# Layer 0 of a two-layer FFT and box-filter kernel: the order of ten matmul rounds, and a seven-row sum on VectorE cut into quarters

## The chip, the cores and the metric

The kernel runs on one core of one Trainium2 chip. The metric is device time of one launch in microseconds, the median of several runs. One launch handles all eight images.

## The reference

The input x has shape (8, 16, 512, 512), float32. Both layers are residual blocks with a group norm (8 groups of 2 channels) in front:

```python
# layer 0: a 3x3 complex convolution in the frequency domain
X = jnp.fft.rfftn(gn(x), axes=(-2, -1)); Xr, Xi = jnp.real(X), jnp.imag(X)
Yr = rconv(Xr, wr) - rconv(Xi, wi) + b_real
Yi = rconv(Xr, wi) + rconv(Xi, wr) + b_imag
x = x + jnp.fft.irfftn(lax.complex(Yr, Yi), axes=(-2, -1))
# layer 1: a 15x15 mean filter, zero padded
x = x + mean_filter(gn(x), 15)
```

A 3x3 convolution of the spectrum is, back in the image, a product with a few sines and cosines of the place. The kernel uses this: it never forms a spectrum.

## The kernel before

**Layout.** The 128 partitions are 8 blocks of image rows times 16 channels, in two halves of 64. An image is 64 "rows" t = 0 to 63 of 128x512 in the tile `img`: row t holds one image row of each of the 8 blocks. After layer 0 a row t in `img` is the layer's output.

**Layer 0, one row n.** TensorE (PE) makes the row's Hilbert transform with 12 matmuls of 128x256 (L536, `front_hilbert`), one row ahead of where it needs it. Then comes `mix`: 40 matmuls of 64x512, in ten rounds of four. The array is used as four 64x64 tiles, so the four of a round run beside each other. Two of a round are "lower" (the operands in partitions 0 to 63, by the list `LOWER`), two are "upper" (partitions 64 to 127, by `UPPER`). They sum three results in PSUM: p0 ("base", with a last "wrap" term, L633), p1 ("cosine") and p2 ("sine"). Each result is opened by one half and closed by the other, three matmul pairs each: p1 is opened by lower cosine and closed by upper cosine, p2 is opened by upper sine and closed by lower sine, and the upper half of p0 is added during the next row's rounds (`late_base`). Between opening and closing PE waits for its own signal: `p1_half` (the last lower cosine pair is done) in front of round 6, `p2_half` (the last upper sine pair is done) in front of round 7. p1 and p2 have one buffer each, so their next opening waits until VectorE has read them: `t1_done` and `t2_done`. Rounds are counted from 0.

VectorE (DVE) takes a row in a "slot": two instructions for the first wave term from p1 (L1264, signal `t1_done`), two for the second from p2 (L1270, `t2_done`), then for the row before it the output row from p0 (L1279, waits for `q_done`) with its statistics (L1282), then the low part of the next row's Hilbert transform (L1222). GpSimd (POOL) makes a row in three additions: the low part of a later normalised row (L1412, f16), wave term 1 plus the image row (L1419), plus wave term 2 (L1422, `q_done`). ScalarE (ACT) normalises, copies the Hilbert transform's high part, and adds a constant to the finished row (`x1_whole`). The order within each engine is the order of the code; semaphores tie the engines.

**Loops.** Every engine runs slots 0 to 7 of a layer unrolled, then a hardware loop of 8 slots each turn, then the last 8 unrolled. On VectorE slots 8 to 15 were unrolled too (`slot(1, s, 1)`), because the head sum stands there. In a loop an instruction that addresses `img` or `bias_c` by row needs register work by the engine's sequencer.

**Head sum.** Layer 1 starts from `head`, the sum of rows 0 to 7. Slots 9 to 15 each end with one addition of 128x512 by `sum_head` (L1298 the first, L1301 the other six). The last one signals `presummed`, for which ScalarE waits after the layer's statistics.

## Time and profile before

| what | value |
|---|---|
| median of 3 runs | 3490.39 us (3487.72 to 3494.23) |
| the profiled execution | 3492.99 us |
| its span, first to last instruction | 3491.0 us |
| PE busy | 3107.4 us (89%) |
| VectorE busy | 3076.4 us (88%) |
| GpSimd busy | 2723.9 us (78%) |
| ScalarE busy | 2446.0 us (70%) |
| granted TensorE clock, mean | 0.980 |

The profile is of one execution. Busy time is the time in which an engine has an instruction in flight; instructions of VectorE overlap by some 0.08 us, so that a start can lie before the end of the one in front. A row of layer 0 takes about 3.8 us, and there are 512 of them. Layer 1 and the work between the layers fill the rest.

### The profile page before, as it was taken

What the parts mean: (1) busy time and instruction counts of PE and PEld (TensorE: products, weight loads), DVE (VectorE), ACT (ScalarE), POOL (GpSimd) and SP (SyncE); (2) the same over time, 40 slices, a digit from 0 to 9 for tenths busy, and PEclk for the clock granted to TensorE, in tenths of its full rate; (3) what the DMA queues carried; (4) which work ended last, traced back from release to release, by engine and by line L of the source; (5) the groups of instructions that cost most, each with busy time, mean ns of one, the idle gap of its engine ahead of it and who ended that gap; (6) DMA issues with size and microseconds to landing.
All of it is one profiled execution on the core that took longest, in us unless ns stands there. A gap on an engine that the chain in (4) does not pass through costs nothing.

```text
span 3491.0 us, 110788 instructions
## 1 busy us (share of the span) xinstructions
PE 3107.4 (89%) x36064; PEld 1869.7 (54%) x36064; DVE 3076.4 (88%) x5786; ACT 2446.0 (70%) x4742; POOL 2723.9 (78%) x2231
## 2 busy tenths in 40 slices
PE   2199979999889988899899998999988999899986
PEld 1155555555555555555555555555555555555555
DVE  6789978999889988899798997999978998889987
ACT  2568865787658876588666885578865787658876
POOL 4079975899749987599776997589974998759986
PEclk9699999999999999999999999999999999999999
DMA  8656668666876659766596666966678665876655
GB/s 206 200 93 128 127 202 252 114 127 120 249 205 126 128 116 285 169 125 128 154 293 125 126 129 184 272 113 128 120 225 229 117 128 119 259 195 126 127 129 174
DMA packets 726765, 573.58 MB, mean 164 GB/s; under 512 B 592416, under 2 KB 667776, under 8 KB 712064
## 3 DMA queue, kind: packets, MB, share of 16 engines
q1 hardware_dynamic: 704000, 451.67, 56.1%
q10 hardware_dynamic: 22400, 117.46, 13.1%
q8 instruction: 178, 2.92, 0.4%
q14 instruction: 187, 1.53, 0.2%
HBM read 262.08 MB, written 148.90 MB: 118 GB/s over the span
## 4 chain that ended last, share of the span: by engine, by line
PE 59%; DVE 16%; issue 9%; POOL 5%; DMA 3%; SPq 3%; ACT 1%; ACTq 1%; DVEq 0%; POOLq 0%
PE p L626 26%; PE h_ps L536 10%; PE h_odd L536 10%; DVE ob_all L1340 6%; DVE arena L1332 4%; PE p L633 4%; POOL arena L1479 3%; PE h_ps L626 3%; DMA out<-ob_all 2%; PE p L768 2%; DVE stat L1102 2%; PE h_ps L633 1%; PE p L575 1%; SPq L371 1%; ACTq L972 1%
## 5 line engine op out<-in xcount | busy, mean ns | idle before, releaser
L626 PE MATMUL p<-arena,bd_all 64*64 64x512 f16 x16896 | 1290.7, 381 | 31.2 <-DVE ob_all L1270 22.2
L626 PEld LDWEIGHTS p<-arena,bd_all 64*64 64x64 f16 x16896 | 555.2, 105 | 374.0 <-issue 233.1
L1419 POOL TENSOR_TENSOR ob_all<-ob_all,img 128x512 f32<-128x512 f32 x512 | 664.5, 1298 | 78.5 <-DVE ob_all L1264 52.2
L1422 POOL TENSOR_TENSOR ob_all<-ob_all 128x512 f32<-128x512 f32 x512 | 654.1, 1277 | 40.1
L1479 POOL TENSOR_TENSOR arena<-img 128x512 f32<-128x512 f32 x392 | 499.0, 1275 | 177.0 <-PE h_ps L757 97.9
L1264 DVE SCALAR_TENSOR_TENSOR ob_all<-p,bias_c,cosw 128x256 f32<-128x256 f32 x1024 | 447.6, 478 | 60.1 <-PE p L626 22.6
L886 ACT ACTIVATE img<-img,half_row (+1 forms) x1024 | 487.7, 528 | 5.0 <-ACT half_row L876 0.4
L768 PE MATMUL p<-band,arena 128*128 128x135 f16 (+1 forms) x4096 | 340.3, 228 | 154.9 <-DVE ob_all L1340 149.8
L1270 DVE SCALAR_TENSOR_TENSOR ob_all<-p,bias_c,cosw 128x256 f32<-128x256 f32 x1024 | 443.2, 474 | 0.0
L1412 POOL TENSOR_TENSOR arena<-arena 128x512 f16<-128x512 f32 x256 | 308.5, 1205 | 160.5 <-ACT arena L860 160.5
L859 ACT ACTIVATE arena<-img,sc 128x512 f16 (+1 forms) x512 | 433.8, 847 | 0.0
L944 ACT ACTIVATE arena<-arena,sc 128x512 f32<-128x512 f32 x392 | 282.9, 722 | 206.6 <-POOL arena L1479 197.9
L1340 DVE SCALAR_TENSOR_TENSOR ob_all<-p,img 128x512 f32<-128x512 f32 x512 | 347.5, 679 | 88.6 <-PE p L768 55.7
L1282 DVE BATCH_NORM_STATS2 stat<-img (+1 forms) x512 | 355.7, 695 | 51.7
L768 PEld LDWEIGHTS p<-band,arena 128*128 128x128 f16 x4096 | 260.5, 99 | 259.1 <-issue 244.6
L575 PE MATMUL p<-img,bd_all 128*64 128x256 f32 x2048 | 300.1, 402 | 92.6 <-POOL bd_all L1383 66.9
L536 PE MATMUL h_ps<-hilbert,arena 128*128 128x256 f16 x3072 | 379.8, 273 | 1.2 <-DMA arena<-arena 1.2
L536 PE MATMUL h_odd<-hilbert,xT_more 128*128 128x256 f16 x3072 | 379.8, 273 | 1.0 <-DMA xT_more<-arena 0.7
L1412 POOL TENSOR_TENSOR arena<-g_more,arena 128x512 f16<-128x512 f32 x256 | 311.7, 1218 | 55.5 <-ACT g_more L860 35.5
L536 PEld LDWEIGHTS h_odd<-hilbert,xT_more 128*128 128x128 f16 x3072 | 279.8, 98 | 138.2 <-issue 91.5
L536 PEld LDWEIGHTS h_ps<-hilbert,arena 128*128 128x128 f16 x3072 | 280.2, 98 | 132.6 <-issue 98.7
L1102 DVE BATCH_NORM_STATS2 stat<-img 128x6 f32<-128x512 f32 x512 | 334.8, 680 | 0.3
(182 smaller groups left out, 5136.6 us busy)
## 6 DMA issues: line engine op xcount, KB each, us to landing
out<-ob_all SPq DMA_DIRECT2D x512, 256.0 KB, 4.5
bd_all<-bd_dram SPq DMA_DIRECT2D x512, 224.0 KB, 2.5
img<-in_x ACTq DMA_DIRECT2D x168, 512.0 KB, 6.9
img<-in_x ACTq DMA_DIRECT2D x112, 256.0 KB, 5.3
img<-in_x SPq DMA_DIRECT2D x24, 512.0 KB, 26.1
arena<-img SPq DMA_DIRECT2D x48, 256.0 KB, 3.2
arena<-img SPq DMA_DIRECT2D x48, 192.0 KB, 2.7
bd_dram<-ob_all SPq DMA_DIRECT2D x11, 768.0 KB, 3.6
```

The source lines that it names most:

```text
L536: m = mm(dst(a), row[:, 4 * lx + k, :], tb["hilbert16"][:, lt, k, 0:cols], start=(half == 0 and i == 0), stop=(half == 1 and i == 2))
L626: m = mm(bank[out_half * HP:(out_half + 1) * HP, :], bd[s % RB][rows, 6 * lm + (j if own else j + 1), :], part, start=opens and i3 == 0, s ...
L768: m = mm(p0[0][:, lo:hi], parts[u % 3][:, l, k, :], tb["band16"][:, lo - k * P + R:hi - k * P + R], start=(u == 0 and k == 0 and l == 0), ...
L859: nc.scalar.activation(halves(gp[s][:, 0, :]), row, ACT.Identity, bias=sc[:, 9:10], scale=sc[:, 8:9])
L886: ins = nc.scalar.activation(row, row, ACT.Identity, bias=half_row[:, s, a:a + 1])
L1264: ins = V.scalar_tensor_tensor(t1[:, a, :], p1[:, a * HALF:(a + 1) * HALF], bias_c[:, 1, t, 1 - a:2 - a], cosw[:, a, :], ALU.subtract, ALU ...
L1270: ins = V.scalar_tensor_tensor(t2[:, a, :], p2[:, a * HALF:(a + 1) * HALF], bias_c[:, 0, t, 1 - a:2 - a], sinw[:, a, :], ALU.add, ALU.mult)
L1340: V.scalar_tensor_tensor(ob[j % NS][:, u % 2, :], p0[0], 1.0 / (K * K * BOX_SCALE), img[:, u, :], ALU.mult, ALU.add).then_inc(row_out, 1)
L1412: G.tensor_tensor(gp[s][:, 1, :], g32[s % 2], gp[s][:, 0, :], ALU.subtract).then_inc(g_split, 1)
L1419: G.tensor_tensor(q, term_row[s % 2][0], parity(img[:, t, :]), ALU.add).then_inc(first_added, 1)
L1422: G.tensor_tensor(q, q, term_row[s % 2][1], ALU.add).then_inc(q_done, 1)
L1479: G.tensor_tensor(diff_row(u), more, less, ALU.subtract).then_inc(moved, 1)
```

## The change

`LOWER` is put in another order: base step 0, then the three cosine steps, then base steps 1 and 2. `UPPER` stays. The wait for `t1_done` moves to round 1, where lower cosine now opens p1; the wait for `t2_done` stays in round 2, where upper sine opens p2. Each has its own signal to `mix_step` (an instruction on PE's sequencer that nobody waits for).

The head sum starts from a memset and becomes 32 additions of 128x128: each slot from 8 to 39 adds one quarter of one row. So four slots handle one row, and the four turns of a new loop handle rows 0 to 7. Slots 8 to 15 are no longer unrolled on VectorE. `presummed` is now signalled by VectorE's sequencer after a wait for all 36 steps.

```diff
-LOWER = [("base", 0), ("base", 1), ("cosine", 0), ("cosine", 1), ("cosine", 2),
+LOWER = [("base", 0), ("cosine", 0), ("cosine", 1), ("cosine", 2), ("base", 1),
          ("base", 2), ("wrap", 3), ("sine", 0), ("sine", 1), ("sine", 2)]
...
-                        if r == min(LOWER.index(("cosine", 0)), UPPER.index(("sine", 0))):
+                        if r == LOWER.index(("cosine", 0)):
                             pe.wait_ge(t1_done, PRIMED + n)
+                            pe.sem_inc(mix_step, 1)
+                        if r == UPPER.index(("sine", 0)):
                             pe.wait_ge(t2_done, PRIMED + n)
                             pe.sem_inc(mix_step, 1)
...
-                def sum_head(t):
-
+                HEAD_OPS = NQ * (R + 2)
+
+                def clear_head():
+
+                    for q in range(NQ):
+                        V.memset(head[:, q * P:(q + 1) * P], 0.0).then_inc(head_chain, 1)
+
+                def sum_head(i, s):
+
+                    t = (i - 1) * (NG // NQ) + s // NQ
+                    cols = slice(s % NQ * P, (s % NQ + 1) * P)
                     dve.wait_ge(x1_whole, b * T + t + 1)
-                    if t == 1:
-                        ins = V.tensor_tensor(head, img[:, 0, :], img[:, 1, :], ALU.add)
-                    else:
-                        dve.wait_ge(head_chain, b * (R - 1) + t - 1)
-                        ins = V.tensor_tensor(head, head, img[:, t, :], ALU.add)
-                    ins.then_inc(head_chain if t < R else presummed, 1)
+                    dve.wait_ge(head_chain, b * HEAD_OPS + (i - 1) * NG + s + 1)
+                    V.tensor_tensor(head[:, cols], head[:, cols], img[:, t, cols], ALU.add).then_inc(head_chain, 1)
...
-                for s in range(NG):
-                    slot(1, s, 1)
-                    if s > 0:
-                        sum_head(s)
-                with dve.Fori(2, T // NG - 1) as i:
+                clear_head()
+                summed = 1 + (R + 1) * NQ // NG
+                with dve.Fori(1, summed) as i:
                     for s in range(NG):
-                        slot(i, s, 2)
+                        slot(i, s, 1)
+                        sum_head(i, s)
+                dve.wait_ge(head_chain, (b + 1) * HEAD_OPS)
+                dve.sem_inc(presummed, 1)
+                with dve.Fori(summed, T // NG - 1) as i:
+                    for s in range(NG):
+                        slot(i, s, summed)
```

What moves on PE, in the rounds of row 1: first the order before. The names are p1 and p2 (in the wave terms), p0_0 for the base of the row before, and h_ps for the base of this row (its buffer lies there); L633 are the wrap terms, round 6.

```order
L626 MATMUL h_ps<-arena,bd_all 64x512 x2
L626 MATMUL p0_0<-arena,bd_all 64x512 x2
L626 MATMUL p1<-arena,bd_all 64x512 [waits t1_done,t2_done]
L626 MATMUL p1<-arena,bd_all 64x512
L626 MATMUL p2<-arena,bd_all 64x512 x2
L626 MATMUL p1<-arena,bd_all 64x512 x2
L626 MATMUL p2<-arena,bd_all 64x512 x2
L626 MATMUL p1<-arena,bd_all 64x512 x2
L626 MATMUL p2<-arena,bd_all 64x512 x2
L626 MATMUL h_ps<-arena,bd_all 64x512 x2
L626 MATMUL p0_0<-arena,bd_all 64x512 x2
L633 MATMUL h_ps<-wrap_row,bd_all 64x512 [waits p1_half]
```

These are the rounds 1 to 6, four matmuls each. The same place now, from the first matmul of round 1:

```order
L626 MATMUL p1<-arena,bd_all 64x512 [waits t1_done]
L626 MATMUL p1<-arena,bd_all 64x512
L626 MATMUL p0_0<-arena,bd_all 64x512 x2
L626 MATMUL p1<-arena,bd_all 64x512 [waits t2_done]
L626 MATMUL p1<-arena,bd_all 64x512
L626 MATMUL p2<-arena,bd_all 64x512 x2
L626 MATMUL p1<-arena,bd_all 64x512 x2
L626 MATMUL p2<-arena,bd_all 64x512 x2
L626 MATMUL h_ps<-arena,bd_all 64x512 x2
L626 MATMUL p2<-arena,bd_all 64x512 x2
L626 MATMUL h_ps<-arena,bd_all 64x512 x2
L626 MATMUL p0_0<-arena,bd_all 64x512 x2
```

The three pairs on p1 stand one round earlier, one pair on h_ps has moved from round 1 to round 4, and p2 stays where it was. L633 with its wait for p1_half follows as before.

On VectorE, the end of a slot with a head sum and the start of the next, before:

```order
L1282 BN_STATS stat<-img 128x6 [waits x1_done]
L1221 REGISTER_ALU
L1222 SCALAR_TENSOR_TENSOR arena<-h_ps,arena 128x512 [waits h_kept]
L1300 REGISTER_ALU [waits x1_whole]
L1301 TENSOR_TENSOR arena<-arena,img 128x512 [waits head_chain]
L1264 SCALAR_TENSOR_TENSOR ob_all<-p1,bias_c,cosw 128x256 [waits p1_ready,q_done]
```

And now, in the loop over slots 8 to 39 (lines are shifted by two to eight):

```order
L1284 BN_STATS stat<-img 128x6 [waits x1_done]
L1223 REGISTER_ALU
L1224 SCALAR_TENSOR_TENSOR arena<-h_ps,arena 128x512 [waits h_kept]
L1308 REGISTER_ALU [waits x1_whole]
L1309 ISA [waits head_chain]
L1309 TENSOR_TENSOR arena<-arena,img 128x128
L1266 ISA [waits p1_ready,q_done]
L1266 SCALAR_TENSOR_TENSOR ob_all<-p1,bias_c,cosw 128x256
```

The addition has a quarter of the columns and stands in 32 slots instead of 7; the rows marked ISA are register work for addresses.

## Rows read from the trace of the kernel before

**Rows 1.** The page: busy us (share of the span) and instructions by engine
```profile
PE 3107.4 (89%) x36064; PEld 1869.7 (54%) x36064; DVE 3076.4 (88%) x5786; ACT 2446.0 (70%) x4742; POOL 2723.9 (78%) x2231
```
**Rows 2.** Image 3 by stretches: length, busy PE, PEld, DVE, ACT, POOL; clock, DMA
```profile
1456.87:1479.80 22.93, 21.52 (x300) 12.16 (x292) 21.63 (x42) 16.63 (x35) 21.27 (x18) 1.00 0.67 115
1479.80:1605.57 125.77, 124.72 (x1669) 71.34 (x1666) 119.39 (x231) 106.15 (x225) 121.14 (x97) 1.00 0.67 126
1605.57:1666.90 61.33, 61.33 (x832) 35.29 (x831) 57.55 (x112) 52.79 (x113) 58.94 (x48) 1.00 0.66 128
1666.90:1697.43 30.53, 29.35 (x410) 17.04 (x408) 28.23 (x57) 21.01 (x52) 27.35 (x24) 1.00 0.56 102
```
**Rows 3.** Timeline of PE (start us, length us): a row in the loop, one unrolled
```profile
1595.35 0.40 PE L626 MATMUL h_ps<-arena,bd_all 64*64 64x512 f16 x2
...
1595.59 0.38 PE L626 MATMUL h_ps<-arena,bd_all 64*64 64x512 f16 x2
...
1596.45 0.40 PE L626 MATMUL h_ps<-arena,bd_all 64*64 64x512 f16 x2
...
1596.79 0.40 PE L633 MATMUL h_ps<-wrap_row,bd_all 64*64 64x512 f16 x2
...
1465.84 1.49 PE L626 MATMUL p<-arena,bd_all 64*64 64x512 f16 x24
1467.26 0.40 PE L633 MATMUL p<-wrap_row,bd_all 64*64 64x512 f16 x2
```
**Rows 4.** Timeline of PE's weight loads in the same looped row
```profile
1595.77 0.39 PEld L626 LDWEIGHTS p<-arena,bd_all 64*64 64x64 f16 x12 [0.28 <-issue]
...
1596.76 0.14 PEld L633 LDWEIGHTS h_ps<-wrap_row,bd_all 64*64 64x64 f16 x2 [0.38 <-issue]
```
**Rows 5.** Timeline of DVE in looped rows
```profile
1594.05 0.88 DVE L1264 SCALAR_TENSOR_TENSOR ob_all<-p,bias_c,cosw 128x256 f32<-128x256 f32 x2
1594.84 0.86 DVE L1270 SCALAR_TENSOR_TENSOR ob_all<-p,bias_c,cosw 128x256 f32<-128x256 f32 x2
1595.62 0.74 DVE L1279 SCALAR_TENSOR_TENSOR img<-p,sc,ob_all 128x512 f32 x1
1596.50 0.69 DVE L1282 BATCH_NORM_STATS2 stat<-img  x1
...
1597.89 0.88 DVE L1264 SCALAR_TENSOR_TENSOR ob_all<-p,bias_c,cosw 128x256 f32<-128x256 f32 x2
```
**Rows 6.** Timeline of DVE in slots with a head sum
```profile
1490.79 0.67 DVE L1222 SCALAR_TENSOR_TENSOR arena<-h_odd,arena 128x512 f16<-128x512 f32 x1
1491.38 0.72 DVE L1301 TENSOR_TENSOR arena<-arena,img 128x512 f32<-128x512 f32 x1
1492.02 0.86 DVE L1264 SCALAR_TENSOR_TENSOR ob_all<-p,bias_c,cosw 128x256 f32<-128x256 f32 x2
...
1495.57 0.78 DVE L1301 TENSOR_TENSOR arena<-arena,img 128x512 f32<-128x512 f32 x1
1496.26 0.47 DVE L1264 SCALAR_TENSOR_TENSOR ob_all<-p,bias_c,cosw 128x256 f32<-128x256 f32 x1
```
**Rows 7.** Timeline of POOL: before and in the head slots, and a looped row
```profile
1483.50 1.16 POOL L1412 TENSOR_TENSOR arena<-arena 128x512 f16<-128x512 f32 x1
...
1491.52 1.60 POOL L1412 TENSOR_TENSOR arena<-arena 128x512 f16<-128x512 f32 x1
...
1596.54 1.27 POOL L1422 TENSOR_TENSOR ob_all<-ob_all 128x512 f32<-128x512 f32 x1
```
**Rows 8.** DVE with POOL idle: small additions (ns: shortest/median/longest), a full one, a memset
```profile
181.29 0.49 DVE L1173 TENSOR_TENSOR kappa<-kappa,trig_h 128x128 f32<-128x128 f32 x2
...
L1173 DVE TENSOR_TENSOR kappa<-kappa,trig_h x16: 282/288/292, 181.3 to 3105.5; 128x128 f32<-128x128 f32 x16
...
191.59 0.69 DVE L1217 TENSOR_TENSOR ob_all<-ob_all 128x512 f32<-128x512 f32 x1
...
2.42 0.30 DVE L1013 MEMSET img<- 128x288 f32 x1
```

## The prediction

> **What bounds the kernel now.** I read the page first: TensorE (PE), VectorE (DVE) and GpSimd (POOL) are all busy 78 to 89% of the span, so the mean names no bound [rows 1]. The change touches only the first layer, 64 rows of each of 8 images, so I cut the layer of one image into stretches at the starts of L1264 (the first wave term of a row) [rows 2]. From one of these starts to the next is one row's period; the starts are those of rows 1, 7, 39, 55 and 63 of image 3. Per row that gives 22.93/6 = 3.82 us, 125.77/32 = 3.93, 61.33/16 = 3.83 and 30.53/8 = 3.82. In the third stretch PE is busy for all of its 61.33 us, DVE for 57.55 and POOL for 58.94: there PE sets the pace, and the others follow 4 to 6% behind. The other images repeat this picture.
>
> PE spends 3.84 us on such a row (the start of L1264 moves from 1594.05 to 1597.89 [rows 5]). Of its ten rounds, counted from 0, round 0 starts at 1595.35 and round 1 at 1595.59 [rows 3]. From round 1 to round 5 (1596.45) it takes 0.86/4 = 0.215 us a round, but from round 5 to round 6 (1596.79) 0.34. Round 6 is where the wrap terms and the second half of the cosine sums start, behind the wait for p1_half; the weight loads show the same hole as 0.38 us of idle in front of L633 [rows 4]. p1_half is signalled by the last lower cosine matmul, in round 4, only two rounds before, and a matmul takes 0.38 to 0.40 us from start to end [rows 3]; what is left over is signal and load. So PE waits 0.34 - 0.215 = 0.12 us of each row for its own pipeline. In an unrolled row (1 to 7 and 55 to 63 are like it) round 6, L633 at 1467.26, comes 1.42 us after round 0, L626 at 1465.84, where an even pace (0.24 for the first step, then five at 0.215) makes 1.32: 0.10 us there [rows 3].
>
> A second loop is as long: t2 ends at 1594.84 + 0.86 = 1595.70, PE loads the weights of round 2 at 1595.77, DVE opens the next row's t1 at 1597.89 and ends its t2 1.65 later at 1599.54, 3.84 us after the last one [rows 4, 5]. The piece of it on PE, rounds 2 to 8, contains the same hole. In the rows 9 to 15, where a whole row is added to the head, DVE is the bound instead: L1264 to L1264 is 4.24 us with no idle time (1492.02 to 1496.26) [rows 6].
>
> **Part 1: the lower order.** It removes nothing and adds one wait with its signal per row on PE's sequencer. Lower cosine moves from rounds 2 to 4 to rounds 1 to 3, so p1_half is signalled a round (0.215 us) earlier and the 0.12 us hole in front of round 6 closes. p2_half stays in round 4 but is wanted only in round 7. Before, its signal came with p1_half, in time for a load at 1596.76 [rows 4], in front of round 6. An even pace would put round 7 at 1596.45 + 0.43 = 1596.88: 0.1 us to spare, so it should not open a hole of its own. The separated waits: t1 has ended at 1594.05 + 0.88 = 1594.93, 0.66 us before round 1, and t2 is still asked for at round 2, as before, so the new wait at round 1 costs nothing; queued behind it on PE are only that round's loads and matmuls. PE's own row falls to 3.72 us, and the loop through t2 as well (3.84 - 0.12).
>
> What is late next? DVE: 57.55/16 = 3.60 busy, 0.14 us in front of L1282 (1595.62 + 0.74 to 1596.50), less the 0.08 us by which L1301 starts before L1222 ends when nothing holds it: 3.66 [rows 2, 5, 6]. POOL: 58.94/16 = 3.68 busy, plus at most the 0.08 us between its two adds, and 0.05 of overlap to win back: 3.71 to 3.76 [rows 2, 7]. POOL may be a little over 3.72, but it may also lag: its sum of a row ends at 1597.81 and DVE wants it for its next L1279, at 1595.62 + 3.84 = 1599.46, 1.65 us later [rows 5, 7]. A few hundredths over some 24 rows fit in, and in the last stretch POOL is idle for 30.53 - 27.35 = 3.2 us in which it can catch up [rows 2]. So I take 3.72 for every row without a head sum. The gain: 6 x 0.10 = 0.6 us in the first stretch; in the third from 61.33 to 16 x 3.72 + 0.1 (a loop's turn) = 59.6, which is 1.7; 7 x 0.10 = 0.7 in the last. Together **3.0 us an image**.
>
> **Part 2: the head sum in quarters.** It removes 7 DVE additions of 128x512 and adds 32 of 128x128 and 4 memsets. Each quarter ends a slot, behind L1222, so DVE then needs 3.66 + q a row; that is above 3.72 for any q over 0.06: all 32 rows become DVE's, and PE's gain is lost in them. The price q: the trace has a 128x128 addition, L1173, of 0.28 us; two take 0.49 together, so the second starts 0.21 after the first, with POOL idle [rows 8]. Beside POOL it costs more: the full addition L1217 takes 0.69 alone, 0.61 without the overlap of 0.08, whereas in the head rows L1301 holds DVE 0.64 (1491.38 to 1492.02) and 0.69 [rows 6, 8]. That adds 0.03 to 0.08, and I don't know whether it shrinks with the size. So q is 0.21 to 0.30; I take 0.26, the small row with the surcharge nearly whole. 32 x (3.66 + 0.26) = 125.4 us. To this come four turns of the loop, for which I take 0.1 each, an estimate from the 0.14 that register work costs in front of L1282 [rows 5], and the memsets: 0.30 for 288 columns, so about 0.15 each for 128 and 0.6 for four [rows 8]. They stand where DVE idles for PE anyhow, (22.93 - 21.63)/6 = 0.2 us a row [rows 2], so 0.4 remains. Sum 126.2 against 125.77: **0.5 us an image lost**, from 1.1 won (q = 0.21) to 1.7 lost (q = 0.30). The waits for x1_whole (a row finished several slots ago) and head_chain (DVE's own addition a slot ago) are met long before, and their register work fits beside L1282 and L1222 (1.3 us). The wait behind the loop, ahead of presummed, costs one drain.
>
> **Sum.** 3.0 - 0.5 = 2.5 us an image, 20 us for eight. The profiled execution took 3492.99 us with a span of 3491.0; it lies 2.6 above the median of 3490.39, and nothing outside the rows changes, so I subtract from the median: **3470**. With the ends of q: 8 x 4.1 = 33 and 8 x 1.3 = 10 us, 3457 to 3480.
>
> **Rivals.** (a) *The hole only moves.* If p2_half reaches the sequencer too late, round 7 waits the 0.10 to 0.12 us that round 6 waited. For it: the 0.1 us to spare is no more than the hole itself, worked out from ends that are modelled. Then Part 1 gives nothing: 3490 + 8 x 0.5 = 3494, and 3504 with q = 0.30. If half of the hole stays, 3482.
>
> (b) *GpSimd pays by the piece, and the kernel gets slower.* Under a full addition L1412 takes 1.60 to 1.61 us instead of 1.16, 0.45 more: it began at 1491.52, and DVE's addition ran from 1491.38 to 1492.10, so it stood still about while DVE added [rows 6, 7]. A quarter should cost it about 0.11. If the price were per instruction, POOL would need 3.75 + 0.45 = 4.20 a row for 32 rows, 134.4 less the lag of 1.65 = 132.8 against 125.8: 7 us an image, 56 - 24 = 32 slower, 3522. It decides from about 0.22 us a quarter (3.75 + 0.22 - 1.65/32 = 3.92). Against it: the 0.45 is within the time that the addition itself runs. The Trainium skill, GPSIMD Engine Reference, section 8, Key points, says that GpSimd shares its SBUF interfaces with VectorE instructions that have two SBUF inputs, as these additions do; by that rule the stall follows the instruction's running time, and the 1.61 beside 1.16 agrees.
>
> (c) *No overlap around the small additions.* If a quarter lets neither neighbour overlap it, q is 0.28 + 0.08 = 0.36: 32 x 4.02 + 0.8 = 129.4, 3.7 lost, 0.7 net, 3496. Against it: the two L1173 overlap by 0.07 us [rows 8]. The Trainium skill, VectorE: DVE Perf Modes, section The DRAIN you can't avoid, says that the next operation does not start until the pipe is empty; it speaks against cutting one addition into four, and would give this case. The overlapping starts of L1173 speak against it here.
>
> **How the numbers follow.** The forecast (hole closed, q 0.21 to 0.30) has 0.66; half of the hole stays, or POOL holds the rows near 3.78, 3481 to 3488, 0.10; rival (a) 0.09; (b) 0.07; (c) 0.05; better than 3457, if some wait goes that I did not see, 0.03. About 0.2% (7 us, 3483.4) is what a measurement of this kernel can tell from no change. Faster by more than that: 0.66 + 0.03 and half of the 0.10, 0.74. Within it: the rest of the 0.10, (c), and (a) with a small q, 0.16. Slower: (b) and part of (a), 0.10. The range for 8 in 10 takes the forecast, the half-closed hole and a little below: 3455 to 3488.
>
> **What would show it.** In the rows 39 to 63 the period should be 3.72 instead of 3.83, with no hole in front of L633's loads (0.38 idle before them would fall to the 0.1 or so of other rounds); a hole that moves to the round after it is (a). In the rows 7 to 39 L1264 to L1264 should be an even 3.90 to 3.95 with DVE hardly idle; 3.96 or more is (c), and a DVE that waits for L1422 with L1412 near 1.6 us in every row is (b). The quarter's duration should be 0.28 to 0.37 us. I am wrong in the whole if DVE's rows come out below 3.85 or PE's above 3.80.

## The result, and the profile after

The changed kernel takes **3463.16 us** (median of 4 runs, 3460.56 to 3468.07), the kernel before 3491.05 beside it (4 runs, 3487.72 to 3494.23). The ratio is 0.9919, with a 95% interval of 0.9907 to 0.9931: 28 us faster, 0.8%. 3470 was predicted, from 3455 to 3488.

The page of the changed kernel (span 3466.0 us, granted clock 0.978) gives nearly the same busy shares in its first row, which answers to [rows 1]:

```profile
PE 3085.5 (89%) x36064; PEld 1877.5 (54%) x36064; DVE 3077.9 (89%) x6018; ACT 2447.4 (71%) x4742; POOL 2713.3 (78%) x2231
```

Cut as in [rows 2], at the starts of the first wave term (now L1266) of rows 1, 7, 39, 55 and 63, an image without a disturbance (image 4) reads:

```profile
1862.61:1885.15 22.54, 21.13 (x302) 12.38 (x299) 22.09 (x46) 16.85 (x36) 21.11 (x18) 1.00 0.64 118
1885.15:2009.19 124.04, 123.74 (x1673) 72.00 (x1672) 118.87 (x257) 106.89 (x225) 120.94 (x97) 1.00 0.68 128
2009.19:2069.28 60.09, 59.62 (x827) 34.88 (x824) 57.48 (x113) 52.06 (x112) 58.03 (x48) 1.00 0.65 129
2069.28:2098.78 29.50, 28.60 (x410) 16.86 (x408) 28.20 (x56) 20.98 (x51) 27.07 (x23) 1.00 0.53 105
```

Against the forecast, as medians over the eight images:

| rows | before | predicted | after |
|---|---|---|---|
| 1 to 7 | 22.92 | 22.3 | 22.55 |
| 7 to 39 (head sum) | 125.76 | 126.2 | 124.20 |
| 39 to 55 | 61.32 | 59.6 | 60.08 |
| 55 to 63 | 30.52 | 29.8 | 29.50 |
| sum | 240.52 | 237.9 | 236.33 |

The forecast had 0.4 for the memsets in the second stretch; they lie at the end of the first. So without them the first stretch would be 22.1.

**The hole in front of the wrap terms is gone.** PE's timeline, rounds 2 to 8 of an unrolled row of after, answers to the last two rows of [rows 3]:

```profile
1449.56 1.05 PE L626 MATMUL p<-arena,bd_all 64*64 64x512 f16 x14 [0.37 <-DVE ob_all L1272]
1450.24 0.38 PE L626 MATMUL h_ps<-arena,bd_all 64*64 64x512 f16 x2
1450.42 0.41 PE L633 MATMUL p<-wrap_row,bd_all 64*64 64x512 f16 x2
```

Round 2 starts at 1449.56 and round 6, L633, at 1450.42: four rounds in 0.86 us, 0.215 each, with nothing left over. In a looped row the weight loads of L633 had 0.38 us of idle before them [rows 4]; now it is 0.16:

```profile
1626.84 0.60 PEld L626 LDWEIGHTS p<-arena,bd_all 64*64 64x64 f16 x16 [0.33 <-issue]
1627.61 0.14 PEld L633 LDWEIGHTS p<-wrap_row,bd_all 64*64 64x64 f16 x2 [0.16 <-issue]
```

**VectorE in the quarter rows** (its timeline in a slot of the new loop, answers to [rows 6]):

```profile
1517.19 0.87 DVE L1266 SCALAR_TENSOR_TENSOR ob_all<-p,bias_c,cosw 128x256 f32<-128x256 f32 x2
1517.97 0.87 DVE L1272 SCALAR_TENSOR_TENSOR ob_all<-p,bias_c,cosw 128x256 f32<-128x256 f32 x2
1518.76 0.74 DVE L1281 SCALAR_TENSOR_TENSOR img<-p,sc,ob_all 128x512 f32 x1
1519.64 0.69 DVE L1284 BATCH_NORM_STATS2 stat<-img  x1
1520.25 0.67 DVE L1224 SCALAR_TENSOR_TENSOR arena<-h_odd,arena 128x512 f16<-128x512 f32 x1
1520.84 0.28 DVE L1309 TENSOR_TENSOR arena<-arena,img 128x128 f32<-128x128 f32 x1
1521.04 0.87 DVE L1266 SCALAR_TENSOR_TENSOR ob_all<-p,bias_c,cosw 128x256 f32<-128x256 f32 x2
```

A row is 1521.04 - 1517.19 = 3.85 us. The quarter runs for 0.28 us, and the next instruction starts 0.20 after it: q = 0.20. The only idle time is the 0.14 in front of L1284. GpSimd's L1423, which begins while the quarter runs, takes 1.21 to 1.30 us in nearly all of the 256 such slots, 1.23 in the median, instead of 1.16 [rows 7].

**Two places cost more than I had thought.** The end of the new loop, in front of row 39's slot:

```profile
1594.07 0.28 DVE L1309 TENSOR_TENSOR arena<-arena,img 128x128 f32<-128x128 f32 x1
1594.96 0.88 DVE L1266 SCALAR_TENSOR_TENSOR ob_all<-p,bias_c,cosw 128x256 f32<-128x256 f32 x2 [0.61 <-DVE arena L1309]
```

and the memsets, in front of row 7:

```profile
1469.15 0.67 DVE L1224 SCALAR_TENSOR_TENSOR arena<-h_ps,arena 128x512 f16<-128x512 f32 x1
1469.80 0.59 DVE L1301 MEMSET arena<- 128x128 f32 x4
1470.31 0.75 DVE L1266 SCALAR_TENSOR_TENSOR ob_all<-p,bias_c,cosw 128x256 f32<-128x256 f32 x2
```

The row that ends in the first takes 4.55 us instead of 3.85, the row that ends in the second 4.12 instead of 3.70.

### The profile page after: what moved, and what is told of

Same layout as the page of the kernel before. It is cut to its first block, busy times and chain, and to the rows that moved or that the text cites. A ratio compares the mean times of both kernels' runs of the same rounds, so it can differ in the third digit from the quotient of the medians.

```text
span 3466.0 us, 112555 instructions
## 1 busy us (share of the span) xinstructions
PE 3085.5 (89%) x36064; PEld 1877.5 (54%) x36064; DVE 3077.9 (89%) x6018; ACT 2447.4 (71%) x4742; POOL 2713.3 (78%) x2231
## 4 chain that ended last, share of the span: by engine, by line
PE 43%; DVE 19%; issue 14%; POOL 10%; SPq 7%; DMA 5%; ACT 1%; ACTq 1%; DVEq 1%; POOLq 0%
PE p L626 19%; PE h_ps L536 7%; PE h_odd L536 7%; DVE ob_all L1351 5%; POOL arena L1490 4%; SPq L417 3%; DVE arena L1343 3%; PE p L770 3%; DMA out<-ob_all 3%; PE h_ps L626 2%; DVE stat L1104 2%; POOL ob_all L1433 2%; DVE ob_all L1272 2%; PE p L633 2%; POOL ob_all L1430 2%
## 5 line engine op out<-in xcount | busy, mean ns | idle before, releaser
L626 PE MATMUL p<-arena,bd_all 64*64 64x512 f16 x16896 | 1263.2, 380 | 25.3 <-DVE ob_all L1266 14.2
L1433 POOL TENSOR_TENSOR ob_all<-ob_all 128x512 f32<-128x512 f32 x512 | 653.4, 1276 | 40.1
L1266 DVE SCALAR_TENSOR_TENSOR ob_all<-p,bias_c,cosw 128x256 f32<-128x256 f32 x1024 | 445.9, 477 | 22.3 <-PE p L626 9.1
L1423 POOL TENSOR_TENSOR arena<-arena 128x512 f16<-128x512 f32 x256 | 309.2, 1208 | 162.0 <-ACT arena L862 162.0
L1284 DVE BATCH_NORM_STATS2 stat<-img (+1 forms) x512 | 355.6, 695 | 58.6
L1423 POOL TENSOR_TENSOR arena<-g_more,arena 128x512 f16<-128x512 f32 x256 | 307.5, 1201 | 58.3 <-ACT g_more L862 38.2
```

The costliest lines, as they stand in the source:

```text
L626: m = mm(bank[out_half * HP:(out_half + 1) * HP, :], bd[s % RB][rows, 6 * lm + (j if own else j + 1), :], part, start=opens and i3 == 0, s ...
L1266: ins = V.scalar_tensor_tensor(t1[:, a, :], p1[:, a * HALF:(a + 1) * HALF], bias_c[:, 1, t, 1 - a:2 - a], cosw[:, a, :], ALU.subtract, ALU ...
L1423: G.tensor_tensor(gp[s][:, 1, :], g32[s % 2], gp[s][:, 0, :], ALU.subtract).then_inc(g_split, 1)
L1433: G.tensor_tensor(q, q, term_row[s % 2][1], ALU.add).then_inc(q_done, 1)
```

## The experiments

Every kernel is compared with the kernel before on its own chip. The runs are from several chips: the kernel before had a median of 3490.13 us beside `order_only`, `quarters_only`, `split_old_order` and `late_signal`, 3492.28 beside `paired_wait`, `no_head`, `order_paired` and `all_three`, and 3492.32 beside the other four. Two kernels from different groups are therefore compared to some 2 us at best. A ratio as recorded can differ from the quotient of the two medians by up to 0.0012. The stretches given are medians over the eight images, in the order of the table above. Where a kernel starts from the changed kernel I say "after", where from the old one "before".

**Theory:** the lower order closes PE's hole, and that is the gain; the quarters cost DVE 0.20 us in 32 rows against 0.4 to 0.5 in 7, and give back a little; the row-38 stop and the split waits take some of it. **Rivals:** the gain comes from the separated waits, or from the spread head sum.

### Each half alone

`order_only`: before, with the new `LOWER` and the separate waits; the whole-row head sum stays.

```diff
-LOWER = [("base", 0), ("base", 1), ("cosine", 0), ("cosine", 1), ("cosine", 2),
+LOWER = [("base", 0), ("cosine", 0), ("cosine", 1), ("cosine", 2), ("base", 1),
...
+                        if r == LOWER.index(("cosine", 0)):
+                            pe.wait_ge(t1_done, PRIMED + n)
+                            pe.sem_inc(mix_step, 1)
```

> The kernel before with the new lower order and the separated waits alone; the head sum stays whole, in slots 9 to 15. Theory (the hole in front of round 6 was the gain, and the quarters take part of it back): the hole is gone in all rows but the seven that VectorE holds at 4.24 us. The unrolled rows fall from 3.83 to 3.70, the looped ones from 3.84 to 3.77 (as seen in the changed kernel, where round 2 starts 0.147 us after t2 ends instead of 0.101), among them the 24 rows 15 to 39, which the quarters hold at 3.86 in the changed kernel. Per image 0.5 + 1.8 + 1.25 + 1.0 = 4.6 us, 37 for eight: about 3454, which is less than the changed kernel's 3463. Rival (both parts are needed, since the gain of the order is only reached where the head sum is spread): no better than 3463.

Measured: 3456.57 us, ratio 0.9896 (0.9880 to 0.9912). It is 34 us faster than before, more than both parts together, where 37 had been expected. Its windows in image 5:

```profile
2271.94:2294.06 22.12, 20.73 (x296) 12.21 (x296) 21.61 (x42) 16.15 (x35) 20.70 (x17) 1.00 0.69 105
2294.06:2417.86 123.80, 121.42 (x1669) 72.38 (x1666) 119.26 (x232) 106.28 (x225) 120.89 (x98) 1.00 0.69 131
2417.86:2477.93 60.07, 60.07 (x833) 35.47 (x831) 57.48 (x112) 52.92 (x113) 58.70 (x49) 1.00 0.65 131
```

The looped rows without a head sum take 3.77 us, the seven with a whole addition 4.24, as before.

`quarters_only`: after, with the old `LOWER` and the joint wait.

```diff
-LOWER = [("base", 0), ("cosine", 0), ("cosine", 1), ("cosine", 2), ("base", 1),
+LOWER = [("base", 0), ("base", 1), ("cosine", 0), ("cosine", 1), ("cosine", 2),
...
-                        if r == LOWER.index(("cosine", 0)):
+                        if r == min(LOWER.index(("cosine", 0)), UPPER.index(("sine", 0))):
```

> The changed kernel with the lower order and the waits of before: the head sum in quarters alone. Theory: VectorE needs 3.66 + 0.20 = 3.86 us in the 32 rows, hardly over the 3.84 that PE needs with its hole, so the rows 7 to 39 take 32 x 3.86 = 123.5, plus 0.7 for the stop at the end of the new loop and 0.4 for the memsets, 124.4 to 124.6 against 125.77: 1.2 us an image, 10 for eight, about 3481. The other stretches stay at 61.3 and 30.5. Rival (a small addition costs 0.26 or more, as I had predicted): 126.2 for the stretch, 3494.

Measured: 3482.43 us, ratio 0.9972 (0.9958 to 0.9987). The second stretch is shorter than before, 124.7 for 125.8, and the first is 0.2 longer by the memsets (23.1 for 22.9); the other two are as before:

```profile
1477.47:1602.30 124.83, 124.25 (x1672) 71.73 (x1670) 118.96 (x258) 106.85 (x225) 120.90 (x97) 1.00 0.68 128
1602.30:1663.63 61.33, 60.79 (x827) 34.66 (x824) 57.58 (x113) 52.12 (x112) 58.25 (x48) 1.00 0.65 127
```

So the quarters win 8 to 10 us over the old order, and lose about 7 over the new one (3463 against 3457): with the hole closed, 3.77 is to be had in the 25 rows that need no head sum, and the quarters hold 32 rows at 3.85.

### The separated waits alone

`split_old_order`: before, the order kept; the wait for `t1_done` stands in round 1 with its own signal.

```diff
-                        if r == min(LOWER.index(("cosine", 0)), UPPER.index(("sine", 0))):
+                        if r == 1:
                             pe.wait_ge(t1_done, PRIMED + n)
+                            pe.sem_inc(mix_step, 1)
+                        if r == UPPER.index(("sine", 0)):
                             pe.wait_ge(t2_done, PRIMED + n)
```

> The kernel before with one edit: the wait for t1_done stands in round 1 with a signal of its own, t2_done stays in round 2, the order of the matmuls and the head sum stay. Theory (a wait for one semaphore costs PE's sequencer 0.05 us after the semaphore has come, a wait that follows another in one instruction does not): round 2 starts 0.147 us after t2's end instead of 0.101, so the 40 looped rows outside the head sum go from 3.84 to 3.89, 1.8 us an image, 15 for eight: 3505. Unrolled rows, where PE does not wait for t2, stay at 3.83. Rival (the 0.046 comes from the order of the matmuls): 3490, no change.

Measured: 3505.30 us, ratio 1.0037 (1.0023 to 1.0050), slower by 15 us. The looped rows go from 3.84 to 3.89, the unrolled ones stay at 3.82:

```profile
1614.83:1676.88 62.05, 62.05 (x832) 35.35 (x831) 57.59 (x112) 52.80 (x113) 58.91 (x48) 1.00 0.65 127
```

So the gain doesn't come from the waits; they cost. What they do is seen in the instruction on PE's weight-load sequencer that signals `mix_step` behind the wait for `t2_done`. The answers are for L696 of before, L698 of after and L699 of the kernel `paired_wait` below; the numbers are shortest/median/longest ns:

```profile
L696 PEldq EVENT_SEMAPHORE  x512: 51/789/791, 194.8 to 3365.5; - x171
```
```profile
L698 PEldq EVENT_SEMAPHORE  x512: 51/51/51, 196.1 to 3340.9; - x171
```
```profile
L699 PEldq EVENT_SEMAPHORE  x512: 51/639/642, 193.8 to 3335.3; - x171
```

I read these durations so: with two waits in front of it the instruction is begun at the first one and sits in flight until t2 is done; with a single wait it begins only when that semaphore has come, and its 51 ns then stand in front of round 2. `paired_wait` tests that: after, with a second wait for `t1_done`, met long before, ahead of the one for `t2_done`.

```diff
                         if r == UPPER.index(("sine", 0)):
+                            pe.wait_ge(t1_done, PRIMED + n)
                             pe.wait_ge(t2_done, PRIMED + n)
```

> The changed kernel with one line more: in round 2 PE waits for t1_done again, which has long come, and then for t2_done, so that the instruction that signals mix_step has two waits in front of it, as it had before the change. Theory (the 0.147 us from t2's end to round 2 are 0.05 of an instruction that only starts when its single semaphore comes; behind a second wait it is started already): 0.101 us again, the looped rows without a head sum fall from 3.77 to 3.72, 16 a image, 0.8 us, 6 for eight: 3457; the 32 rows with a quarter stay at 3.86, since VectorE holds them. Rival (the extra time belongs to two signals to mix_step in a row, or to the loads' new place): 3463.

Measured: 3460.91 us, ratio 0.9907 (0.9890 to 0.9923), and the looped rows that DVE doesn't hold are as expected, 3.72 us. Its third stretch, and t2 with the load of round 2 in one row (DVE and the weight loads):

```profile
1592.40:1651.91 59.51, 59.04 (x827) 34.91 (x825) 57.15 (x112) 52.03 (x112) 57.59 (x48) 1.00 0.65 130
```
```profile
1622.99 0.86 DVE L1273 SCALAR_TENSOR_TENSOR ob_all<-p,bias_c,cosw 128x256 f32<-128x256 f32 x2
```
```profile
1623.92 0.60 PEld L626 LDWEIGHTS p<-arena,bd_all 64*64 64x64 f16 x16 [0.28 <-issue]
```

t2 ends at 1623.85 and the load starts 0.07 later, as before (1595.70 to 1595.77 [rows 4, 5]). In after, t2 ends at 1625.86 + 0.87 = 1626.73 and the load follows at 1626.84, 0.11 later. Round 2's first matmul starts 0.147 us after t2's end in after and 0.102 here. An added wait that is always met makes each of these rows 0.05 us shorter. It does so only where PE waits for t2 and VectorE isn't the bound, in the 16 rows 39 to 54: their stretch falls from 60.08 to 59.50. That should be 5 us for eight images, and 3457 was expected. The 3460.91 don't show it: they are 2 us under after, inside the interval of the ratio, and the profiled execution lost two images' time to a fallen clock (below), after one. The rows are shown, the gain in time isn't.

### What the head sum costs

`no_head`: after, without the 32 additions, so that the head sum stays zero; that part of the computation is left out.

```diff
                         slot(i, s, 1)
-                        sum_head(i, s)
-                dve.wait_ge(head_chain, (b + 1) * HEAD_OPS)
+                dve.wait_ge(head_chain, (b + 1) * NQ)
```

> The changed kernel without the 32 additions; the memsets stay, so the head sum is zero and this part of the computation is left out. Theory (the quarters hold VectorE, and nothing else holds the rows 7 to 39): these rows fall from 3.86 to the 3.77 of the others, 32 x 0.085 = 2.7 us an image, 22 for eight: 3441. Rival (the new loop, its register work or GpSimd holds them): they stay near 3.86 and the time at 3463.

Measured: 3438.18 us, ratio 0.9848 (0.9826 to 0.9869). The looped rows take 3.77 but for the turn at row 14 (below). The price of the whole head sum in after is 25 us. By the second stretch it is 3.0 an image (124.20 less 121.16): 31 rows by 0.085, which is 2.6, and the stop, 4.55 for 3.77 in row 38, make 3.4; PE's waits for DMAs, a little longer here, hide some of it (row 14 is 4.14 here, 4.06 in after). Row 38 has lost its stop although the wait for the memsets still stands there: what costs is a wait for an instruction that is still running, and not the change of loops.

`late_signal`: after, with the wait for the last quarter and the signal `presummed` moved behind the second loop.

```diff
-                dve.wait_ge(head_chain, (b + 1) * HEAD_OPS)
-                dve.sem_inc(presummed, 1)
                 with dve.Fori(summed, T // NG - 1) as i:
                     for s in range(NG):
                         slot(i, s, summed)
+                dve.wait_ge(head_chain, (b + 1) * HEAD_OPS)
+                dve.sem_inc(presummed, 1)
```

> The changed kernel with the wait for head_chain and the signal presummed moved from the end of the summing loop to the end of the following loop. Theory (VectorE's row 38 takes 4.55 us instead of 3.86 because its sequencer must wait for the last quarter to end before it may start the next loop's register work): row 38 falls to about 3.86, 0.6 to 0.7 us an image, 5 for eight: 3458. Rival (the change of loops itself costs it): 3463, row 38 stays.

Measured: 3455.07 us, ratio 0.9888 (0.9869 to 0.9906), 8 us better than after where 5 were expected. The second stretch is 0.89 us shorter in each image (123.31 for 124.20), which is 7 for eight. Row 38 gives 0.70 of it. The rest is row 14, at the first turn of the new loop: its median is 4.06 us in after and 3.86 here. In after PE waits there for the DMAs of the transposed rows in five of eight images, by 0.2 to 1.1 us, here in one. I hadn't expected that, and why it comes in that row, and more often in after, is open. VectorE at the same place, without the stop:

```profile
1588.43 0.28 DVE L1309 TENSOR_TENSOR arena<-arena,img 128x128 f32<-128x128 f32 x1
1588.63 0.87 DVE L1266 SCALAR_TENSOR_TENSOR ob_all<-p,bias_c,cosw 128x256 f32<-128x256 f32 x2
```

Row 38 is 3.85 instead of 4.55. The wait for DVE's own last instruction had kept the next loop's register work from running under it; that the register work is what fills the 0.61 us is argued, that the wait causes them is shown.

`halves`: after with the late signal and the paired wait, and the head sum in 16 additions of 128x256 in slots 8 to 23.

```diff
...
-                    t = (i - 1) * (NG // NQ) + s // NQ
-                    cols = slice(s % NQ * P, (s % NQ + 1) * P)
+                    t = (i - 1) * (NG // NH2) + s // NH2
+                    cols = slice(s % NH2 * 2 * P, (s % NH2 + 1) * 2 * P)
...
```

> As the kernel with the late signal and the paired wait, but with 16 additions of 128x256 in slots 8 to 23, two memsets. Theory (a piece holds VectorE 0.07 us and 0.13 for each 128 columns: 0.20 for a quarter as measured, so 0.33 for a half, 0.60 to 0.65 for a whole): 16 rows at 3.66 + 0.33 = 3.99 and 16 at 3.72 are 123.4 for the rows 7 to 39, as 32 at 3.86 are 123.4: no difference to the quarters, 3449. Rival (a small piece has no price of its own, only its columns count): the halves would be worse than the quarters only by the slack they waste, and a half would measure 0.39 or more.

Measured: 3450.64 us, ratio 0.9888 (0.9868 to 0.9907). Here is VectorE around a half:

```profile
1071.47 0.42 DVE L1311 TENSOR_TENSOR arena<-arena,img 128x256 f32<-128x256 f32 x1
1071.80 0.87 DVE L1267 SCALAR_TENSOR_TENSOR ob_all<-p,bias_c,cosw 128x256 f32<-128x256 f32 x2
```

(In these lines, and in `paired_wait` above, t1 is L1267 because of the added line.) A half holds DVE 0.33 us, a quarter 0.20, a whole row 0.63 to 0.71 (two of them in [rows 6]). Summed over a row of the image that is 0.80 in quarters, 0.66 in halves and about 0.67 whole. Against a row of 3.72 that DVE could nearly keep (3.66), each slot with a piece loses q - 0.06: 32 x 0.14 = 4.5 us an image in quarters and 16 x 0.27 = 4.3 in halves. The slots with a whole addition are unrolled and don't have the idle time in front of the statistics, so they take 4.24 and lose 0.52 each, 7 x 0.52 = 3.6. The second stretches agree: 123.26 us in `late_paired` (quarters), 123.21 in `halves`, 122.84 in `order_paired_again` (whole). The pieces also need their memsets in the first stretch, 22.5 against 22.1. So the whole additions are the cheapest by 0.8 us an image, since DVE has only those 0.06 us a row to give.

### Why round 4 was early enough, and round 5 is not

`p2_late`: `order_only` with upper sine's last pair in round 5 instead of 4, two rounds ahead of round 7, where p2_half is wanted.

```diff
...
-UPPER = [("base", 0), ("base", 1), ("sine", 0), ("sine", 1), ("sine", 2),
-         ("base", 2), ("cosine", 0), ("cosine", 1), ("cosine", 2), ("wrap", 3)]
+UPPER = [("base", 0), ("base", 1), ("sine", 0), ("sine", 1), ("base", 2),
+         ("sine", 2), ("cosine", 0), ("cosine", 1), ("cosine", 2), ("wrap", 3)]
```

> The kernel with the new lower order and the whole head sum, but with the last upper sine pair moved from round 4 to round 5, so that p2_half is signalled two rounds ahead of round 7, as p1_half was of round 6 in the kernel before. Theory (a signal of PE to itself needs more than two rounds, less than three): a hole of 0.10 to 0.12 us in front of round 7 in every row, the unrolled rows back from 3.70 to 3.82, the looped from 3.77 to 3.87 to 3.89, some 56 rows an image outside the seven head slots by 0.11, 6 us, 49 for eight: 3500 to 3506. Rival (only p1 was the matter, since the wrap terms follow it): 3457.

Measured: 3510.97 us, ratio 1.0046 (1.0032 to 1.0061). The weight loads show the hole in front of round 7, 0.31 us of idle, where after has none that the view marks:

```profile
1645.15 0.11 PEld L626 LDWEIGHTS p<-arena,bd_all 64*64 64x64 f16 x2
1645.56 0.38 PEld L626 LDWEIGHTS p<-arena,bd_all 64*64 64x64 f16 x10 [0.31 <-issue]
```

3500 to 3506 was expected, so it cost 5 us more than I had thought. One pair of matmuls moved by one round costs 52 to 54 us against `order_only` (18.7 slower than its kernel before, where `order_only` is 33.6 faster). The hole is 0.12 us in unrolled rows and 0.14 in looped ones (0.334 and 0.356 from round 6 to round 7, less 0.215), where before had 0.10 and 0.12 in front of round 6; the rows are 3.84 and 3.90. The explanation of the gain is thereby shown from the other side: in these rounds of 0.215 us a signal three rounds ahead of its use leaves no hole, one two rounds ahead opens it, for either of the two sums. It also sizes what was to spare in round 4: 0.215 less 0.12 to 0.14, which is 0.08 to 0.10 us.

### Kernels put together

`order_paired` and `order_paired_again` are the same kernel: `order_only` with the paired wait. `late_paired` is after with the late signal and the paired wait. `all_three` moves the memsets too, into the slot in which the first row is finished.

```diff
                         if r == UPPER.index(("sine", 0)):
+                            pe.wait_ge(t1_done, PRIMED + n)
                             pe.wait_ge(t2_done, PRIMED + n)
```

> The kernel before with the new lower order, the head sum whole as before, and in round 2 the two waits, t1_done again and t2_done. Theory: 3.72 instead of 3.77 in the 40 looped rows outside the head slots, 2.0 us an image, 16 for eight from the 3457 of the order alone: 3441, the fastest so far. Rival (another engine, GpSimd at 3.71 to 3.76 or the transposing DMAs, takes over): 3450 or more.

Measured: 3448.30 us, ratio 0.9868 (0.9851 to 0.9884): 7 us more than expected.

> The kernel with the new order, the paired wait and the whole head sum once more, on the same chip as the two with pieces: 3448, equal to them within 3 us (theory), or 4 and more slower than them (rival).

Measured: 3446.86 us, ratio 0.9870 (0.9852 to 0.9889). This is the fastest kernel that computes the whole result, 45 us faster than before and 16 to 18 faster than after. The time is as expected, but both sides of the comparison with the pieces missed: on the same chip it is 4 us faster than `halves` and 9 faster than `late_paired`, where equal or slower had been expected. By the stretches given with `halves` it should be some 6 for both; `late_paired` lost some 3 more to its fallen clock (below). The intervals of the three ratios overlap, so the order of the three is shown by the stretches and only suggested by the times.

> The changed kernel with the late signal and the paired wait of round 2, the memsets where they were. Theory: 5 less than the 3455 of the late signal, 3449 to 3450, like the 3448 of the whole additions with the same two waits: 32 rows at 3.86 and one memset stop cost what 7 rows at 4.24 cost (both about 4 us an image over 3.72). Rival (quarters are the better way once their stop is gone): 3444 or less.

Measured: 3455.49 us, ratio 0.9897 (0.9881 to 0.9913): 5 us more than expected.

```diff
+                    if t == 2:
+                        clear_head()
                     if t >= 2:
...
-                clear_head()
                 summed = 1 + (R + 1) * NQ // NG
```

> The changed kernel with three edits: the late signal, the paired wait in round 2, and the four memsets moved into slot 2, between the wave terms and the first output row, where VectorE waits 2.4 us for GpSimd in each image. Theory: from the 3455 of the late signal, row 6 falls from 4.12 to 3.75 (0.4 us an image, 3 for eight), the 16 rows of paired_wait give 6: 3446. Rival (the memsets' place costs nothing, row 6 is slow for the entry into the loops): 3449.

Measured: 3452.17 us, ratio 0.9877 (0.9857 to 0.9897): 6 us more than expected. Here I had misread a view. The waits of DVE list 18.9 us for "DVE img L1281 <- POOL ob_all L1433", 2.4 us in each image, and I took it for the first finished row, where the memsets would then cost nothing. It belongs to the last row of an image. Row 6 became 0.3 shorter and rows 1 and 2 together as much longer: the memsets cost 0.3 to 0.4 wherever DVE sets the pace.

**What was missing in three of them, and a clock that falls.** `order_paired`, `late_paired` and `all_three` had the expected length in their looped rows, and still came out 5 to 7 us too long. In the profiles of all kernels with the new order something else is seen in row 1 that the kernel before doesn't have. These are PE's timeline and the windows of `order_paired` in image 3 (the last three numbers of a window are the granted clock, the share and the GB/s of the DMAs):

```profile
1440.22 0.40 PE L626 MATMUL h_ps<-arena,bd_all 64*64 64x512 f16 x2
1442.01 0.40 PE L626 MATMUL p<-arena,bd_all 64*64 64x512 f16 x2 [1.39 <-DVE ob_all L1267]
...
1442.75 1.26 PE L626 MATMUL p<-arena,bd_all 64*64 64x512 f16 x14 [0.33 <-DVE ob_all L1273]
...
1445.67 2.05 PE L536 MATMUL h_ps<-hilbert,arena 128*128 128x256 f16 x12
...
1449.93 1.48 PE L536 MATMUL h_odd<-hilbert,xT_more 128*128 128x256 f16 x12
```
```profile
1442.00:1443.40 1.40, 1.06 (x17) 0.58 (x20) 1.37 (x4) 0.39 (x1) 1.32 (x2) 1.00 0.66 102
1443.40:1447.65 4.25, 4.25 (x37) 2.28 (x29) 3.46 (x7) 0.00 (x0) 3.51 (x3) 0.60 0.29 69
1447.65:1451.00 3.35, 3.35 (x51) 2.09 (x51) 2.49 (x6) 2.45 (x5) 2.55 (x4) 1.00 0.46 72
```

PE waited 1.39 us for the first wave term of row 1, did the four matmuls of round 1, waited 0.33, and a little later the granted clock fell: 0.60 as the mean of the next 4.25 us, so most of them at 1.2 GHz, and 1.00 (2.4 GHz) from then on. The 12 Hilbert matmuls took 2.05 us instead of 1.48, and rows 1 to 7 took 1.64 us longer (23.72 instead of 22.08). This occurred in three of the eight images of `order_paired`, and in two of the same kernel's second profile; in three of `late_paired`, in four of `all_three` and of `order_only`, in two of `paired_wait`, and in one each of after (its image 0, 24.18 instead of 22.55), `late_signal`, `no_head` and `halves`. Over the ten profiles of kernels with the new order (without `p2_late`, whose hole is back), 22 of 80 images have it. All 22 are among the 48 in which the wait in front of round 1 is 1.33 us or longer; none of the 32 with a shorter wait has it. Before, PE has one wait there of 1.38 to 1.79 us, then works without a stop, and the clock falls in none of its eight images, nor in the eight of `quarters_only`:

```profile
1458.63 1.05 PE L626 MATMUL p<-arena,bd_all 64*64 64x512 f16 x14 [1.41 <-DVE ob_all L1270]
```

The falls account for the missing time only in part. `late_paired` and `all_three` were forecast from `late_signal`, whose profile has one of them; theirs have three and four, 3 to 4 us more. `order_paired` was forecast from `order_only`, whose profile has four, and it has three, its second profile two; so they can't be what it lacks. There the rows 1 to 63 of all images went from 1893.0 us to 1879.7 and 1876.3, so they won 13 and 17 us, or 12 and 13 without the falls, where 16 had been expected. More is missing in the rest of the span, 1564.6 us in `order_only` and 1572.1 and 1568.5 here, which scatters from kernel to kernel (below). How many falls there are in the executions without a profile isn't known.

I take the fall as shown by the clock's own rows, and its cause, the stop that the new order cuts in two by the four matmuls of round 1, as argued. `split_old_order` and `p2_late` cut it as well, but there the wait never exceeds 1.22 us and the clock doesn't fall, so no run holds the length of the wait fixed and changes only the cut. Why it comes in 22 of the 48 images and not in all is open.

## Why the prediction was right, and where its steps were off

The direction and the size were right, and so was the main reason: 3470 predicted, 3463 measured. That the two are so near is in part luck: several terms inside were off and went opposite ways, and in the profiled executions 31 us were won in the rows, where 20 had been forecast, and 6 lost outside them (the sum, below).

**Part 1, the hole.** Right: it closed in full, and didn't move to round 7 (rival (a)). `order_only` shows that this part makes the whole gain. That p2_half in round 4 is just in time, "0.1 us to spare", is borne out by `p2_late`: a round later the hole is back, and its size leaves 0.08 to 0.10 us.

**Part 1, the separated waits.** Wrong: "the new wait at round 1 costs nothing". I had asked only whether t1 would be done in time and who is queued behind the wait. The cost is in the other wait, which lost its companion, and so 0.046 us came between t2 and round 2 in each looped row. The looped rows are 3.77 instead of 3.72, 60.08 instead of 59.6 in the third stretch. The unrolled rows came to 3.70 instead of 3.72, and the row behind the loop won 0.20, so the last stretch won 1.0 instead of 0.7, and the first, without the memsets, 0.8 instead of 0.6 (`order_only`: 22.1). In sum Part 1 gave 0.8 + 1.2 + 1.0 = 3.0 us an image, as forecast, by two errors that cancel: that the sum came out is luck.

**Part 2, the price of a quarter.** The base of 3.66 was right. q was mis-sized: 0.26 taken, 0.20 measured (3.66 + 0.20 = 3.86, and 3.85 is seen). The surcharge beside GpSimd doesn't exist for a piece so small: 0.28 us with GpSimd busy, and 0.28 with it idle [rows 8]. That is 32 x 0.06 = 1.9 us an image of the difference. The four loop turns, for which I had 0.4, cost nothing in themselves: rows 22 and 30 take 3.85 like the others, and row 14 does wherever PE doesn't wait for a DMA. L1266 starts 0.08 us before the quarter ends, so rival (c) fell. The Trainium skill, VectorE: DVE Perf Modes, section The DRAIN you can't avoid, says that the next operation doesn't start until the pipe has emptied, but also that one that isn't held starts earlier. The prediction left out that second half, and these pairs agree with it.

**Part 2, the stop.** "The wait behind the loop, ahead of presummed, costs one drain" was the second mis-sized term. It took 0.70 us in each image, 5.6 in all (`late_signal` takes it out). I take it that behind it the register work of the next loop stands in front of an engine that has run dry. The memsets took 0.42 of row 6, where I had 0.4. With the memsets moved to the first stretch, the forecast for rows 7 to 39 was 125.8; less 1.9 for q and 0.4 for the turns, plus 0.7 for the stop, it is 124.2, which is what was measured, though the 0.2 that row 14 lost to DMAs is in the measured one and no term of mine.

**GpSimd, rival (b).** False. The stall follows the time that the addition runs: 0.45 under a whole row, 0.05 to 0.14 under a quarter of 0.28 us, 0.07 in the median, where I had taken 0.11. The Trainium skill, GPSIMD Engine Reference, section 8, Key points, has the rule that these engines share their SBUF interfaces for instructions with two SBUF inputs, and the rows agree with it in kind.

**The sum.** 240.52 - 236.33 is 4.2 us an image by medians, 33.5 for eight. The rows 1 to 63 of all images really went from 1925.5 to 1894.2 us, 31.3 less: image 0 lost 1.6 to the fallen clock, and single rows lost some to DMAs that bring the transposed rows for the Hilbert transform. PE's waits in before and in after (us in total, times, longest):

```profile
PE h_ps L536 <- DMA arena<-arena: 1.2, 1, 1.2
```
```profile
PE h_ps L536 <- DMA arena<-arena: 7.0, 9, 1.2
```

The rest of the span, layer 1 and what lies between, was 1565.5 us and is 1571.8. It lies between 1559 and 1572 in the profiles of this study, and doesn't follow the edits. 31.3 - 6.3 = 25.0 is the difference of the two spans.

**The ranges.** Rows below 3.85 for DVE or above 3.80 for PE would have meant that I was wrong in the whole. They came out at 3.85 and 3.77, both near to the mark. At 3.84 the first sign would have called the whole wrong while its main reason held, so it was set too tight. The head rows, for which 3.90 to 3.95 was forecast, lie below that by the error of q.

## What to carry to other kernels

Where an engine waits for a signal of its own pipeline, count the rounds between the last instruction that signals and the first that needs it: here two rounds of 0.215 us left a hole of 0.10 to 0.14, and three left none, which was worth 34 us of 3490 for moving one step of base matmuls behind the three cosine steps, the last of which signals. Work that is cut into pieces and spread over many rows wins only if the engine has slack in those rows that is larger than a piece; here it had 0.06 us for pieces of 0.20, so cutting it won nothing: whole additions cost least, by the memsets and by 0.4 us an image in the rows, and the stop at the loop's edge came on top. An engine's wait for itself at the edge of a loop belongs where the engine idles anyway.

## What the hardware showed that I had not expected

- A semaphore instruction of PE's sequencer behind a single wait delays the matmul after it by 0.046 us more than one that stands behind two, the first already met: from t2's end to the load of round 2 0.11 us against 0.07, and its median duration is 51 ns against 639 to 789.
- TensorE's granted clock fell to its lower level in row 1 of 22 of 80 images with the new order, after waits of 1.33 to 1.39 us and 0.33 to 0.38 with four matmuls between them; it cost 1.64 us each time, 1.3 in `all_three`. A single wait of up to 1.79 us in the same place never did it in the eight images of before or the eight of `quarters_only`.
- A 128x128 addition holds VectorE 0.20 us and runs 0.28, with GpSimd busy or idle; a 128x256 one holds it 0.33, a 128x512 one 0.63 to 0.71 beside GpSimd.
- PE's waits for the transposing DMAs in front of the `h_ps` matmuls rose from 1.2 us in before to 7.0 in after. Shorter rows alone don't explain it: `order_only` has them too, and 2.4 us; `quarters_only` keeps the long rows, and has 4.8. Why is open.
